# Squares of queries and keys: from ScalarE to GpSimd, for the fifth sequence and later ones

## The chip, the cores and the metric

One Trainium2 chip, one of its cores. The metric is the device time of one execution in microseconds, as the median of several runs. A core has five engines with instruction queues of their own that meet at semaphores: TensorE (PE in the profile; PEld is its weight load), VectorE (DVE), ScalarE (ACT), GpSimd (POOL) and SyncE (SP), which here issues transfers.

## The reference

The input `x` holds 16 sequences of 256 tokens with 128 features. Three layers run one after the other, each on the layer norm of its input: half of a mixture of 8 experts (128 to 512 to 128, one expert for each token), an attention with 16 heads of width 8, and half of the mixture of experts once more. The change lies in the attention's treatment of queries and keys:

```python
q = (x @ wq.T).reshape(B, T, H, hd); k = ...; v = ...
def rms(t):
    var = jnp.mean(t * t, axis=-1, keepdims=True) + EPS
    return g_rms * (t * jax.lax.rsqrt(var))
q, k = (rms(q), rms(k))
q, k = (rope(q), rope(k))
scores = einsum(q, k) * scale + 1.0
y = softmax(scores) @ v
```

`t * t` are the squares of which this document speaks: 128 tokens on the partitions, 256 values (queries and keys of 16 heads) in the free dimension, twice for a sequence (`tt` 0 and 1). The rope turns each half of a head by an angle and commutes with the factor of `rms`, so the kernel turns the raw values and scales them later.

## The kernel before

The program is written out by hand: each engine runs its own list, and the place of a call in a function `step(n)` sets the order. Three stages follow one another: the first mixture of experts (39 tiles of 128 tokens), the attention, and the second mixture.

In the attention each engine runs `step(n)` for n from -20 to 68; step n of TensorE computes the scores of group n, which is a quarter (4 heads) of sequence n // 4. So four steps make one sequence, and a step is known by n mod 4. The same step also works ahead for later groups. For sequence b:

- Normalised input: `xn(b)` on VectorE at step 4b - 20, two instructions that read `X` and `Rstd` from SBUF.
- TensorE projects queries, keys and values of the first 128 tokens at step 4b - 16 and of the other 128 at 4b - 14 (`project_qkv`, L920).
- ScalarE empties the result: `qkv_square` (L1251) writes the squares `Sq`, and `qkv_copy` writes `QkRaw` and `Vg`. The first half is handled at the end of step 4b - 16, the second half's squares at the end of step 4b - 14 and its copies inside step 4b - 13.
- GpSimd's `rope(b, tt)` reads `QkRaw`: a product with `RopeA` (L675), two half-width products with `RopeB` (L680), for `tt` 1 a small one (L687), and the sum of the two (L691). It stands at steps 4b - 16 and 4b - 14; at the latter `split` of sequence b - 1 (L703, L710) comes ahead of it.
- VectorE's `sums(b)` (L1705) adds the squares of each head, at step 4b - 13, and frees ScalarE's `inverse_root(b)` at step 4b - 11. `normalise(b)` (L1715, writes `Rn`) follows at 4b - 10, and GpSimd's `split(b)` waits for it.

The other work of a step n, as the steps of the prediction name it:

- TensorE: scores (L977), scores without a maximum for group n + 6 in two pairs (L954), values of group n - 1 (L1001), and transposes of queries and keys of group n + 7 (L936). The transposes wait for VectorE's first maximum of that step, and the scores of the next step for ScalarE's copy of the transposes.
- ScalarE: two exponentials (L1218), copy of the transposed queries and keys (`QkT`, L1122), small copies.
- VectorE: two maxima (L1732) of 128x1024 from PSUM, and one or two other things. In a step with n mod 4 = 0: `xn`, then `residual` (L1753, L1754), which takes the attention's output for the sequence that is ready. In a step with n mod 4 = 2: `normalise`, at n = 6, 14, 22 and 30 behind four `bn_stats` of reloaded tiles.
- GpSimd: gathers of later tiles (`fetch`, L638, each with a pause L600), and from n = 43 on stores of finished tiles (`place`, L620). The layer norm terms of the second lot of finished tiles (L655 to L665, n = 45) and its router logits (L718 to L723, n = 48) stand there too; VectorE's `one_hot` of step 49 (L1416) waits for the latter.

Of the kernel before, what the change touches and what calls it, by code (L numbers as in the profile page):

```python
# [5 lines left out]
P = 128  # L6
SEQ_TILES = 2
# [77 lines left out]
DRAIN_FIRST = {1: (65,)}  # L85
DRAIN_SECOND = {2: (66, 67), 3: (68,)}
LAST = {"norm": 3, "inverse": 6, "logits": 4, "rank": 9}
XN_AT = {-20: 0, -16: 1, -10: 2, -8: 3, -2: 4}
GATHER_STEP = [0, 1, 2, 3, 4, 5, 6, 9, 10, 13, 14, 17, 18, 21, 22, 25]

def program(nc, x, wqkvT, wpT, g_rms, wrT, br, w1T, b1, w2T, b2,
            ident, before, ones, expert_rank, tile_start, rope_cos, rope_sin, out):
    F32, F32R, I32, BF16 = mybir.dt.float32, mybir.dt.float32r, mybir.dt.int32, mybir.dt.bfloat16
    ALU, ACT, AX = mybir.AluOpType, mybir.ActivationFunctionType, mybir.AxisListType.X
# [11 lines left out]
    with ctx:  # L106
        def sb(name, shape, dt=F32):
            return ctx.enter_context(nc.sbuf_tensor(name, shape, dt))
# [4 lines left out]
        def sem(name):  # L113
            return ctx.enter_context(nc.semaphore(name))
# [100 lines left out]
        QkRaw = sb("QkRaw", [P, 2, SEQ_TILES, 2 * P + N_EXP])  # L215
        Vg = sb("Vg", [P, R_V, SEQ_TILES, N_GRP, GH * 32 + HD + 1])
        Sq = sb("Sq", [P, 2, 2, SEQ_TILES, P])
# [96 lines left out]
        emptied7 = sem("emptied7")  # L314
        qkT_ps = sem("qkT_ps")
        qkT_ready = sem("qkT_ready")
        ss_ready = sem("ss_ready")
        ln_ready = sem("ln_ready")
        rr_ready = sem("rr_ready")
# [29 lines left out]
        def lot(j):  # L349

            return 1 if j < 2 else 2 + j // CH if j >= CH else 2
# [6 lines left out]
        def group(m):  # L358
            return 0 <= m < N_ALL

        def seq(n, lead):

            b, r = divmod(n + lead, N_GRP)
            return b if r == 0 and 0 <= b < N_SEQ else -1
# [39 lines left out]
        def bank_of(*key):  # L404
            return where[key][0]

        def filled(*key):
            return FILLED[where[key][0]], where[key][1]

        def emptied(*key):  # L410
            return EMPTIED[where[key][0]], where[key][1]
# [28 lines left out]
        def tile_expert(k, t):  # L440

            return (Exp2I if k and t >= FULL else ExpI)[0:1, t:t + 1]
# [117 lines left out]
        def _(pool):  # L560
# [106 lines left out]
            def rope(b, tt):  # L667
                u = b % 2
                pool.wait_ge(*emptied(f"qkv{tt}", b))
                if b >= 2:  # L670
                    pool.wait_ge(rn_ready, b - 1)
                if b >= 1:
                    pool.wait_ge(rot_ready, SEQ_TILES * (b - 1) + tt + 1)
                heads = QkRaw[:, u, tt, 0:2 * P].rearrange("p (q h d) -> p q h d", q=2, d=HD)
                nc.gpsimd.tensor_tensor(Rot[:, u, :, tt, :].rearrange("p q (h d) -> p q h d", d=HD), heads,  # L675
                                        RopeA[:, tt].unsqueeze(2).to_broadcast([P, 2, N_HEAD, HD]), ALU.mult)
                half = HD // 2
                swapped = RotB[:, :, tt, :].rearrange("p q (h d) -> p q h d", d=HD)
                for a, c in ((0, half), (half, 0)):
                    last = nc.gpsimd.tensor_tensor(swapped[:, :, :, a:a + half], heads[:, :, :, c:c + half],  # L680
                                                   RopeB[:, tt, :, a:a + half].unsqueeze(2).to_broadcast([P, 2, N_HEAD, half]),
                                                   ALU.mult)
                last.then_inc(rot_terms, 1)
                if tt == 1:
                    j = SEQ_TILES * b
                    pool.wait_ge(std_ready, lot(j))
                    nc.gpsimd.tensor_tensor(Lg[:, j:j + SEQ_TILES, :], QkRaw[:, u, :, 2 * P:2 * P + N_EXP],  # L687
                                            Std[:, j:j + SEQ_TILES].unsqueeze(2).to_broadcast([P, SEQ_TILES, N_EXP]),
                                            ALU.mult).then_inc(logit_in, 1)
                pool.wait_ge(rot_terms, 2 * b + tt + 1)  # L690
                nc.gpsimd.tensor_tensor(Rot[:, u, :, tt, :], Rot[:, u, :, tt, :], RotB[:, :, tt, :], ALU.add).then_inc(rot_ready, 1)  # L691
# [78 lines left out]
            for t in range(S_TILES):  # L770
                if t == LAST["norm"]:
                    lot_layernorm(N_LOT + 1 + LAST_LOT)
                if t == LAST["logits"]:
                    lot_logits(LAST_LOT)
# [7 lines left out]
        def _(pe):  # L782
# [56 lines left out]
            def experts(k):  # L839
# [42 lines left out]
                for t in range(S_TILES + 1):  # L882
# [7 lines left out]
                    if t >= 1:  # L890
                        e = pe.value_load(tile_expert(k, t - 1), min_val=0, max_val=N_EXP - 1)
                    if k and t == LAST["rank"]:
                        rank(LAST_LOT)
# [226 lines left out]
        def _(act):  # L1120
            def copy(dst, src):
                return nc.scalar.activation(dst, src, ACT.Copy)  # L1122
# [23 lines left out]
            def experts(k):  # L1146
# [33 lines left out]
                def run():  # L1180
                    x_evacuate(0)
                    for t in range(S_TILES):
# [6 lines left out]
                        relu(t)  # L1189
                        if k and t == LAST["inverse"]:  # L1190
                            inverse_deviation(N_LOT + len(ROUTE_LOTS))
# [54 lines left out]
            def qkv_square(b, tt):  # L1246
                act.wait_ge(*filled(f"qkv{tt}", b))
                if b >= 2:
                    act.wait_ge(ss_ready, b - 1)
                qk = PS[:, bank_of(f"qkv{tt}", b), 0:2 * P].rearrange("p (q d) -> p q d", q=2)  # L1250
                nc.scalar.activation(Sq[:, b % 2, :, tt, :], qk, ACT.Square)  # L1251

            def qkv_copy(b, tt):
                if b >= 2:
                    act.wait_ge(rot_ready, 2 * (b - 2) + 2)
                if b >= R_V:
                    act.wait_ge(*filled("yu", 2 * (b - R_V) + 1))
                copy(QkRaw[:, b % 2, tt, :], PS[:, bank_of(f"qkv{tt}", b), 0:2 * P + N_EXP])
                copy(Vg[:, b % R_V, tt, :, 0:GH * 32].rearrange("p k (h r) -> p k h r", r=32)[:, :, :, 0:HD],
                     PS[:, bank_of(f"qkv{tt}", b), 2 * P + N_EXP:3 * P + N_EXP].rearrange("p (k h d) -> p k h d", k=N_GRP, d=HD)).then_inc(emptied(f"qkv{tt}", b)[0], 1)  # L1260
# [15 lines left out]

            def first_copy(n):
                if seq(n, 16) >= 0:
                    qkv_square(seq(n, 16), 0)
                    qkv_copy(seq(n, 16), 0)  # L1280

            def second_square(n):
                if seq(n, 14) >= 0:
                    qkv_square(seq(n, 14), 1)

            def second_copy(n):
# [76 lines left out]
        def _(dve):  # L1363
# [335 lines left out]

            def sums(b):  # L1700
                u = b % 2
                dve.wait_ge(*emptied("qkv1", b))
                if b >= 2:
                    dve.wait_ge(rr_ready, b - 1)
                nc.vector.tensor_reduce(Ss[:, u], Sq[:, u].rearrange("p q t (h d) -> p (q t h) d", d=HD),  # L1705
                                        AX, ALU.add).then_inc(ss_ready, 1)
# [61 lines left out]
            def step(n):  # L1768
                if n in RANK_AT:
                    lot_take(RANK_AT[n])  # L1770
                if group(n + MAX_LEAD) and n >= 0:
                    maxima(n + MAX_LEAD, 0)
                if not late(n):
                    small_take(n)
                if late(n) and seq(n - 1, -8) >= 0:
                    residual_stats(seq(n - 1, -8))
                if group(n + MAX_LEAD):
                    maxima(n + MAX_LEAD, 1)
                if n < 0:
                    if n in XN_AT:  # L1780
                        xn(XN_AT[n])
                elif seq(n, 20) >= 0:
                    xn(seq(n, 20))
                if late(n):
                    small_take(n)
                if n in STATS_AT:
                    reload(STATS_AT[n])
                    if STATS_AT[n] < POOL_LOTS:
                        layernorm(STATS_AT[n])
                if seq(n, 13) >= 0:  # L1790
                    sums(seq(n, 13))
                if n in PLACE_AT:
                    lot_place(PLACE_AT[n])
                if n in NORM_AT:
                    layernorm(N_LOT + 1 + NORM_AT[n])
                if n in LOGITS_AT:
                    lot_logits(LOGITS_AT[n])
                if n in HOT_AT:
                    if HOT_AT[n] < len(POOL_LOGITS_AT):
                        dve.wait_ge(lg_ready, HOT_AT[n] + 1)  # L1800
                    one_hot(slice(*ROUTE_LOTS[HOT_AT[n]]))
                if n in PICK_AT:
                    pick(slice(*ROUTE_LOTS[PICK_AT[n]]))
                if n in SEEN_AT:
                    lot_seen(SEEN_AT[n])
                if norm_seq(n) >= 0:
                    normalise(norm_seq(n))
                if n == TABLE_AT:
                    full_table()
# [167 lines left out]
```

## Time and profile before

| | |
|---|---|
| median of 3 runs | 493.08 us (492.8 to 496.94) |
| profiled execution | 493.35 us |
| its span, first to last instruction | 491.5 us |
| PE busy | 433.9 us, 88% |
| DVE busy | 380.5 us, 77% |
| POOL busy | 358.6 us, 73% |
| ACT busy | 349.3 us, 71% |
| chain that ended last, by engine | PE 39%, DVE 19%, POOL 18%, issue 13%, ACT 7% |

Busy time is a sum over the whole program and says little on one stage. The chain follows the last instruction back to what released it, at each step. The attention's steps 0 to 64 lie between 149 and 396 us of the span.

### The profile page before, as it was taken

What the parts mean: (1) busy time and instruction counts of PE and PEld (TensorE: products, weight loads), DVE (VectorE), ACT (ScalarE), POOL (GpSimd) and SP (SyncE); (2) the same over time, 40 slices, a digit from 0 to 9 for tenths busy, and PEclk for the clock granted to TensorE, in tenths of its full rate; (3) what the DMA queues carried; (4) which work ended last, traced back from release to release, by engine and by line L of the source; (5) the groups of instructions that cost most, each with busy time, mean ns of one, the idle gap of its engine ahead of it and who ended that gap; (6) DMA issues with size and microseconds to landing.
All of it is one profiled execution on the core that took longest, in us unless ns stands there. A gap on an engine that the chain in (4) does not pass through costs nothing.

```text
span 491.5 us, 14012 instructions
## 1 busy us (share of the span) xinstructions
PE 433.9 (88%) x4108; PEld 322.8 (66%) x4108; DVE 380.5 (77%) x1037; ACT 349.3 (71%) x782; POOL 358.6 (73%) x579
## 2 busy tenths in 40 slices
PE   7998999969888989999999998988797979799994
PEld 4348998758665555656566655665464459789994
DVE  4785788758787788898988889888788647777772
ACT  4316776757745789999999898888666856557671
POOL 8028898999968588878684874399747616889985
PEclk9798999989997899999999999999899889999998
DMA  7962335251100000000000000000001123223210
GB/s 196 275 255 51 92 89 150 61 164 37 35 24 16 8 25 15 13 8 8 14 14 2 3 3 3 2 13 17 22 25 35 35 57 79 67 84 90 69 37 6
DMA packets 28649, 27.02 MB, mean 55 GB/s; under 512 B 5684, under 2 KB 25947, under 8 KB 28018
## 3 DMA queue, kind: packets, MB, share of 16 engines
q1 hardware_dynamic: 24034, 17.65, 12.1%
q0 software_dynamic: 4544, 8.49, 6.3%
q8 instruction: 36, 0.59, 0.5%
q14 instruction: 35, 0.29, 0.2%
HBM read 16.56 MB, written 12.71 MB: 60 GB/s over the span
## 4 chain that ended last, share of the span: by engine, by line
PE 39%; DVE 19%; POOL 18%; issue 13%; ACT 7%; DMA 1%; DVEq 1%; SPq 1%; ACTq 1%; POOLq 1%
DVE Smax L1732 8%; PE PS L1001 7%; PE PS L860 7%; PE PS L876 6%; PE PS L954 5%; POOL out L629 5%; PE PS L977 4%; POOL Unread L600 4%; PE PS L936 3%; DVE St L1375 2%; ACT Pt L1218 2%; PE PS L920 2%; POOL Pt L607 2%; POOL XX L638 1%; ACT QkT L1122 1%
## 5 line engine op out<-in xcount | busy, mean ns | idle before, releaser
L1732 DVE TENSOR_REDUCE Smax<-PS 128x4 f32<-128x1024 f32 x128 | 155.7, 1223 | 36.3 <-PE PS L954 35.5
L1218 ACT ACTIVATE Pt<-PS 128x1024 f32<-128x1024 f32 x128 | 126.4, 1024 | 20.2 <-PE PS L977 16.9
L876 PE MATMUL PS<-W,HsT 128*128 x624 | 87.4, 284 | 5.7 <-ACT HsT L1163 2.0
L860 PE MATMUL PS<-XsT,Ws 128*128 128x128 f32 x624 | 85.6, 282 | 2.4 <-ACT XsT L1122 2.0
L876 PEld LDWEIGHTS PS<-W,HsT 128*128 128x128 f32 x624 | 77.7, 196 | 10.5 <-issue 9.1
L860 PEld LDWEIGHTS PS<-XsT,Ws 128*128 128x128 f32 x624 | 79.0, 197 | 5.3 <-ACT XsT L1122 2.6
L1001 PE MATMUL PS<-Pt,Vg 128*32 128x256 f32 x1024 | 72.8, 404 | 0.2
L703 POOL TENSOR_TENSOR HL<-Rn,Zero 128x512 fp32r<-128x512 f32 x28 | 35.3, 1282 | 41.8 <-DVE Rn L1715 40.3
L954 PE MATMUL PS<-QkT 24*128 24x256 f32 x512 | 61.3, 312 | 3.0 <-DVE Smax L1732 2.0
L600 POOL MEMSET Unread<- 128x352 f32 (+1 forms) x140 | 62.0, 443 | 0.1
L607 POOL DMA_INDIRECT Pt<-rows,TokI x39 | 40.6, 1040 | 28.6 <-DVE TokI L1573 20.4
L1616 DVE TENSOR_SCALAR HsT<-PS,Bs 128x128 f32<-128x128 f32 x144 | 43.7, 345 | 22.6 <-PE PS L860 21.6
L954 PEld LDWEIGHTS PS<-QkT 24*128 24x128 f32 x512 | 41.3, 190 | 30.1 <-ACT Pt L1218 24.4
L1122 ACT ACTIVATE Ws<-W 128x512 f32 x78 | 49.0, 631 | 10.6 <-DVE ExpI L1580 6.7
L1122 ACT ACTIVATE XsT<-PS 128x128 f32<-128x128 f32 x78 | 21.7, 278 | 46.8 <-PE PS L849 46.6
L1163 ACT ACTIVATE HsT<-PS,Bs 128x128 f32<-128x128 f32 x168 | 51.4, 366 | 4.6 <-PE PS L860 4.5
L629 POOL DMA_INDIRECT out<-AtCol x39 | 38.6, 989 | 21.7 <-DVE AtCol L1627 15.1
L1122 ACT ACTIVATE QkT<-PS 128x512 fp32r<-128x512 f32 x64 | 38.4, 600 | 19.6 <-PE PS L936 18.8
L977 PE MATMUL PS<-QkT 25*128 25x256 f32 x512 | 34.8, 337 | 18.7 <-DVE Smax L1732 9.5
L936 PE MATMUL PS<-I,HL 128*128 128x128 f32 x256 | 43.3, 293 | 6.7 <-DVE Smax L1732 4.5
L977 PEld LDWEIGHTS PS<-QkT 25*128 25x128 f32 x512 | 22.4, 191 | 34.3 <-issue 32.1
L620 POOL DMA_INDIRECT slots<-XX,SlotI x32 | 31.7, 991 | 17.4 <-ACT Pt L1218 12.7
(251 smaller groups left out, 726.4 us busy)
## 6 DMA issues: line engine op xcount, KB each, us to landing
AtCol<-slots SPq DMA_DIRECT2D x39, 65.5 KB, 1.8
rows<-XX SPq DMA_DIRECT2D x8, 288.0 KB, 4.3
XX<-x SPq DMA_DIRECT2D x8, 256.0 KB, 5.1
W<-w1T SPq DMA_DIRECT2D x2, 1024.0 KB, 6.1
W<-w2T SPq DMA_DIRECT2D x2, 1024.0 KB, 9.3
mid<-mid_second SPq DMA_DIRECT2D x1, 1472.0 KB
mid<-Ys SPq DMA_DIRECT2D x16, 64.0 KB
QkT<-NmaxT SPq DMA_DIRECT2D x64, 4.0 KB
```

The source lines that it names most:

```text
L600: nc.gpsimd.memset(Unread[:, 0:columns], 0.0).then_inc(paused, 1)
L629: pool.indirect_dma_start(out, bass.IndirectOffsetOnAxis(ap=Xs2[:, t % R_X2, P + 2:P + 3].bitcast(I32), axis=0), Xs2[:, t % R_X2, 0:P], No ...
L860: last = nc.tensor.matmul(PS[:, h_bank(n) + c // 2, (c % 2) * P:(c % 2 + 1) * P], Ws[:, n % R_WS, c * P:(c + 1) * P], XsT[:, n % 2, :], st ...
L876: last = nc.tensor.matmul(PS[:, y_bank(n), 0:P], HsT[:, n % 2, c, :], W2[:, ds(e * D_FF + c * P, P)], start=(c == 0), stop=(c == FC - 1))
L936: last = nc.tensor.transpose(PS[:, qkT_bank(m), qk * T + tt * P:qk * T + (tt + 1) * P], v, I[:])
L954: last = nc.tensor.matmul(PS[:, max_bank(m, pair) + h % 2, tt * T:(tt + 1) * T], QkT[rows, m % R_QK, 0, tt * P:(tt + 1) * P], QkT[rows, m ...
L977: last = nc.tensor.matmul(PS[:, score_bank(m, h // 2) + h % 2, c * T:(c + 1) * T], QkT[rows, m % R_QK, 1, c * P:(c + 1) * P], QkT[rows, m ...
L1001: last = nc.tensor.matmul(PS[32 * h:32 * h + 32, 6, 0:T], weights[:, c, at:at + 32], Pt[:, m % 2, h, c, :], start=(m % 2 == 0 and c == 0), ...
L1122: return nc.scalar.activation(dst, src, ACT.Copy)
L1163: last = nc.scalar.activation(HsT[:, n % 2, c, :], PS[:, h_bank(n) + c // 2, (c % 2) * P:(c % 2 + 1) * P], ACT.Relu, bias=Bs[:, n % 2, c:c ...
L1218: nc.scalar.activation(Pt[:, m % 2, 2 * pair:2 * pair + 2, :, :].rearrange("p h c t -> p (h c t)"), PS[:, score_bank(m, pair):score_bank(m ...
L1732: nc.vector.tensor_reduce(Smax[:, b % 2, :, at:at + 33:32].rearrange("p t h -> p h t"), PS[:, max_bank(m, pair):max_bank(m, pair) + 2, :]. ...
```

## The change

For sequences from the fifth on (`b >= 4`), ScalarE no longer squares; GpSimd squares `QkRaw` inside `rope`, between the products and the sum. VectorE's `sums(b)` waits for the two squares on GpSimd and stands at step 4b - 12 in place of 4b - 13, behind `xn` and `residual` of that step. `qkv_copy` takes over the wait for the projection that `qkv_square` had.

```diff
+ACT_SQUARES = 4
 def rope(b, tt):                                       # GpSimd
     ...
                 last.then_inc(rot_terms, 1)
+                if b >= ACT_SQUARES:
+                    pool.wait_ge(ss_ready, b - 1)
+                    qk = QkRaw[:, u, tt, 0:2 * P].rearrange("p (q d) -> p q d", q=2)
+                    nc.gpsimd.tensor_tensor(Sq[:, u, :, tt, :], qk, qk, ALU.mult).then_inc(sq_ready, 1)
                 if tt == 1:
 def qkv_copy(b, tt):                                   # ScalarE
+    if b >= ACT_SQUARES:
+        act.wait_ge(*filled(f"qkv{tt}", b))
 def first_copy(n):
     if seq(n, 16) >= 0:
-        qkv_square(seq(n, 16), 0)
+        if seq(n, 16) < ACT_SQUARES:
+            qkv_square(seq(n, 16), 0)
         qkv_copy(seq(n, 16), 0)
 def second_square(n):
-    if seq(n, 14) >= 0:
+    if 0 <= seq(n, 14) < ACT_SQUARES:
 def sums(b):                                           # VectorE
-    dve.wait_ge(*emptied("qkv1", b))
+    if b < ACT_SQUARES:
+        dve.wait_ge(*emptied("qkv1", b))
+    else:
+        dve.wait_ge(sq_ready, SEQ_TILES * (b - ACT_SQUARES + 1))
 # in VectorE's step(n), behind xn and residual:
-    if seq(n, 13) >= 0:
+    if 0 <= seq(n, 13) < ACT_SQUARES:
         sums(seq(n, 13))
+    if seq(n, 12) >= ACT_SQUARES:
+        sums(seq(n, 12))
```

VectorE, one sequence from `normalise` (step n mod 4 = 2) to the first maximum of the step n mod 4 = 1, before:

```order
L1715 TENSOR_TENSOR Rn<-Rot,Rr 128x512 [waits hl_ready,rot_ready,rr_ready]
L1732 TENSOR_REDUCE Smax<-PS 128x2x2 [waits filled6,smax_ps] x2
L1705 TENSOR_REDUCE Ss<-Sq 128x64 [waits rr_ready,emptied7]
L1732 TENSOR_REDUCE Smax<-PS 128x2x2 [waits filled6,smax_ps] x2
L1695 SCALAR_TENSOR_TENSOR XN<-XX,Mean 128x128 [waits filled7,ln_rstd]
L1695 SCALAR_TENSOR_TENSOR XN<-XX,Mean 128x128
L1753 TENSOR_TENSOR XX<-PS,XX 128x2x128 [waits logit_in,filled6]
L1754 TENSOR_TENSOR Lg<-PS,Lg 128x16
L1732 TENSOR_REDUCE Smax<-PS 128x2x2 [waits filled6,smax_ps]
```

and now (line numbers are those of the changed kernel):

```order
L1727 TENSOR_TENSOR Rn<-Rot,Rr 128x512 [waits hl_ready,rot_ready,rr_ready]
L1744 TENSOR_REDUCE Smax<-PS 128x2x2 [waits filled6,smax_ps] x4
L1704 SCALAR_TENSOR_TENSOR XN<-XX,Mean 128x128 [waits filled7,ln_rstd]
L1704 SCALAR_TENSOR_TENSOR XN<-XX,Mean 128x128
L1765 TENSOR_TENSOR XX<-PS,XX 128x2x128 [waits logit_in,filled6]
L1766 TENSOR_TENSOR Lg<-PS,Lg 128x16
L1717 TENSOR_REDUCE Ss<-Sq 128x64 [waits rr_ready,sq_ready]
L1744 TENSOR_REDUCE Smax<-PS 128x2x2 [waits filled6,smax_ps]
```

The sum of squares left the place between two pairs of maxima and stands between the residual and the next step's first maximum.

GpSimd, the rope part of the second 128 tokens and the gather behind it, before:

```order
L675 TENSOR_TENSOR Rot<-QkRaw,RopeA 128x2x128 [waits rot_ready,rn_ready,emptied7]
L680 TENSOR_TENSOR RotB<-QkRaw,RopeB 128x2x16x4 x2
L687 TENSOR_TENSOR Lg<-QkRaw,Std 128x16 [waits std_ready]
L691 TENSOR_TENSOR Rot<-Rot,RotB 128x2x128 [waits rot_terms]
L638 DMA XX<-mid,SlotI 128x128
```

and now:

```order
L677 TENSOR_TENSOR Rot<-QkRaw,RopeA 128x2x128 [waits rot_ready,rn_ready,emptied7]
L682 TENSOR_TENSOR RotB<-QkRaw,RopeB 128x2x16x4 x2
L689 TENSOR_TENSOR Sq<-QkRaw 128x2x128 [waits ss_ready]
L693 TENSOR_TENSOR Lg<-QkRaw,Std 128x16 [waits std_ready]
L697 TENSOR_TENSOR Rot<-Rot,RotB 128x2x128 [waits rot_terms]
L640 DMA XX<-mid,SlotI 128x128
```

One product is added, and everything behind it on GpSimd comes later by it.

## Rows read from the trace of the kernel before

**Rows 1.** Busy time by stretch: PE, PEld, DVE, ACT, POOL, then granted clock, DMA.

```profile
240.60:255.80 15.20, 13.80 (x163) 8.78 (x161) 13.55 (x20) 13.86 (x28) 12.94 (x26) 1.00 0.05 13
```

**Rows 2.** Timeline of PE, steps 24 to 26: start, us, engine, line, [idle before].

```profile
247.21 0.63 PE L1031 MATMUL PS<-Wp,YnT 128*128 128x136 f32 x4
247.77 0.51 PE L977 MATMUL PS<-QkT 25*128 25x256 f32 x8
...
249.99 0.66 PE L936 MATMUL PS<-I,HL 128*128 128x128 f32 x4
...
251.54 0.51 PE L977 MATMUL PS<-QkT 25*128 25x256 f32 x8 [0.45 <-DVE Smax L1732]
```

**Rows 3.** Timeline of ACT, the same steps.

```profile
247.41 0.38 ACT L1251 ACTIVATE Sq<-PS 128x256 f32<-128x256 f32 x1
...
248.33 1.94 ACT L1218 ACTIVATE Pt<-PS 128x1024 f32<-128x1024 f32 x2
250.69 0.60 ACT L1122 ACTIVATE QkT<-PS 128x512 fp32r<-128x512 f32 x1 [0.41 <-PE PS L936]
```

**Rows 4.** Timeline of DVE, steps 23 to 25.

```profile
243.41 0.67 DVE L1705 TENSOR_REDUCE Ss<-Sq 128x64 f32<-128x512 f32 x1
244.74 1.23 DVE L1732 TENSOR_REDUCE Smax<-PS 128x4 f32<-128x1024 f32 x1 [0.65 <-PE PS L954]
246.17 1.23 DVE L1732 TENSOR_REDUCE Smax<-PS 128x4 f32<-128x1024 f32 x1 [0.21 <-PE PS L954]
247.31 0.77 DVE L1695 SCALAR_TENSOR_TENSOR XN<-XX,Mean 128x128 f32<-128x128 f32 x2
...
248.34 0.16 DVE L1754 TENSOR_TENSOR Lg<-PS,Lg 128x16 f32<-128x16 f32 x1
248.55 1.23 DVE L1732 TENSOR_REDUCE Smax<-PS 128x4 f32<-128x1024 f32 x1
```

**Rows 5.** Timelines of POOL, DVE and PE, steps 20 and 21.

```profile
231.01 0.72 POOL L691 TENSOR_TENSOR Rot<-Rot,RotB 128x256 f32<-128x256 f32 x1
...
233.20 0.16 DVE L1754 TENSOR_TENSOR Lg<-PS,Lg 128x16 f32<-128x16 f32 x1
233.53 1.23 DVE L1732 TENSOR_REDUCE Smax<-PS 128x4 f32<-128x1024 f32 x1 [0.17 <-PE PS L954]
...
234.90 0.63 PE L936 MATMUL PS<-I,HL 128*128 128x128 f32 x4
```

**Rows 6.** Timeline of POOL, rope of the second 128 tokens beside rows 4.

```profile
245.30 0.74 POOL L675 TENSOR_TENSOR Rot<-QkRaw,RopeA 128x256 f32<-128x256 f32 x1
245.99 0.78 POOL L680 TENSOR_TENSOR RotB<-QkRaw,RopeB 128x128 f32<-128x128 f32 x2
...
246.89 0.74 POOL L691 TENSOR_TENSOR Rot<-Rot,RotB 128x256 f32<-128x256 f32 x1
```

**Rows 7.** Timelines of DVE and POOL in the ramp, short windows.

```profile
144.04 0.41 DVE L1695 SCALAR_TENSOR_TENSOR XN<-XX,Mean 128x128 f32<-128x128 f32 x1
144.38 0.88 DVE L1695 SCALAR_TENSOR_TENSOR XN<-XX,Mean 128x128 f32<-128x128 f32 x1
144.38 0.72 POOL L691 TENSOR_TENSOR Rot<-Rot,RotB 128x256 f32<-128x256 f32 x1
```

**Rows 8.** Chain that ended last, POOL's first and last pieces, then DVE: start, us.

```profile
318.88 2.52 POOL HL L703 x2
...
344.61 0.29 POOL Lg L723
344.92 0.23 DVE Mx L1416
```

**Rows 9.** Timeline of DVE, where that piece hands over.

```profile
344.92 0.22 DVE L1416 TENSOR_REDUCE Mx<-Lg 128x8 f32<-128x64 f32 x1 [0.68 <-POOL Lg L723]
```

**Rows 10.** Timelines of DVE, step 38, and PE, step 41.

```profile
298.35 2.35 DVE L1732 TENSOR_REDUCE Smax<-PS 128x4 f32<-128x1024 f32 x2
...
310.09 0.18 PE L824 MATMUL PS<-SeenE,Ahead 128*128 128x8 bf16 x1 [0.21 <-DVE Lg L1754]
```

**Rows 11.** Busy time by stretch, behind that hand-over, columns as in rows 1.

```profile
352.00:358.00 6.00, 5.54 (x41) 3.45 (x40) 2.57 (x3) 3.19 (x5) 5.43 (x8) 0.50 0.07 22
```

More of the change, by code:

```diff
@@ L316, in program @@
         qkT_ready = sem("qkT_ready")
+        sq_ready = sem("sq_ready")
         ss_ready = sem("ss_ready")
```

## The prediction

> **What bounds the kernel now.** I read the chain that ended last first: between 149 and 318 us it changes from engine to engine several times in a step, so no engine is the bound by itself. The busy times by stretch say the same [rows 1]: of 15.2 us for four steps TensorE is busy for 13.80, ScalarE 13.86, VectorE 13.55, GpSimd 12.94. So the question is which wait ends last at the places that the change touches, and for that I read the timelines engine by engine, for a sequence's four steps (24 to 27, and 20 to 23, the two kinds that alternate).
>
> A step of TensorE begins with the scores L977. Step 25's start at 247.77 and follow L1031, which ends at 247.84 and overlaps by 0.07: here TensorE runs through and waits for nobody [rows 2]. Step 26's start at 251.54. That row names VectorE, but ScalarE's copy QkT ends at 251.29 [rows 3], 0.25 before it; that copy itself sat idle for 0.41 until TensorE's transposes L936, which run from 249.99 on. The transposes need VectorE's first maximum of the step, which runs from 248.55 to 249.78 [rows 4], so only 0.21 us before they start. The loop to watch is therefore: VectorE's first maximum of the step with n mod 4 = 1, transposes, copy, next scores. Whatever delays that maximum by more than 0.21 delays all engines.
>
> Late in the attention there is another bound. From 318.88 to 344.90 the chain is GpSimd alone [rows 8], and VectorE waits 0.68 for it at the end [rows 9].
>
> **What ScalarE saves.** 24 squares of 0.38 us [rows 3], 9.1 us of busy time. In the first step of a sequence the square stands at 247.41, and two copies and the next exponentials at 248.33 follow it. These need the scores that started at 247.77 and took 0.51, until 248.28 [rows 2]; without the square ScalarE would wait for them, and 0.05 is gained at most. In the third step the square stands behind the copy QkT for which TensorE waits. So I take nothing for it; the bounds are 0 and the 9.1.
>
> **What GpSimd gains in work.** The trace shows no square on GpSimd. The nearest row is the product of the same size, L675: it starts at 245.30 and the next instruction at 245.99, so 0.69 each [rows 6]. The half-width product takes 0.39 (0.78 for two), a lower bound; the double-width L703 takes 1.26 [rows 8], an upper one. I take 0.69. While GpSimd has idle time in each sequence the 24 x 0.69 = 16.6 us are covered, and two things are left.
>
> First, the **late chain**. Three squares lie in it: the second half of sequence 14 (step 42) and both halves of sequence 15 (steps 44 and 46). 3 x 0.69 = 2.1 us, with 1.2 and 3.8 as bounds. All of it arrives, since VectorE already waits there. The sums of steps 44 and 48 run in that wait: sums of step 48 has to wait for sequence 15's second square, but what it loses is less than the 2.1 by which GpSimd is late anyway. If this cover were gone they would cost some 0.5 each. [...]
>
> Second, **XN beside GpSimd**. In the ramp one XN that starts together with L691 takes 0.88 and ends at 145.26, 0.16 after L691's end at 145.10; the XN just before it took 0.41 [rows 7]. So an XN does not get through while such an instruction runs. In step 24 the pair of XN starts at 247.31 and ends at 248.08 [rows 4], while L691 runs until 247.63 [rows 6]. With the square L691 starts 0.69 later and ends at 248.32; the second XN would end at 248.48, 0.40 later than now. The Trainium skill (SBUF — State Buffer, section on the two separate sides) states this as a rule: a VectorE instruction with two SBUF inputs and a GpSimd instruction that reads SBUF exclude each other for a whole instruction. By that rule the trace agrees, 0.88 against 0.41, and it speaks against this change; without it the sum below would be 2.0 us smaller (five steps of 0.40).
>
> **What VectorE's move costs.** Sums leaves a place where it costs nothing: it runs for 0.67 from 243.41, and behind it VectorE is idle for 0.65 until TensorE's scores arrive [rows 4]. It goes to the place ahead of the first maximum of the loop above. An instruction on VectorE starts 0.09 before the end of the one ahead (247.31 against 246.17 + 1.23), so sums adds 0.58, and starts 0.07 after Lg.
>
> - Steps 8, 16, 24 and 32 (four tiles are reloaded two steps ahead of each, and the rope runs late, into XN): the maximum moves from 248.55 to 248.34 + 0.40 + 0.07 + 0.58 = 249.39, 0.84 later. Less the 0.21 of slack, 0.63 arrive. Four times: 2.5 us.
> - Steps 12, 20 and 28: L691 ends at 231.73 [rows 5], with the square at 232.42, about where XN begins, so XN is left alone. The maximum moves from 233.53 to 233.20 + 0.07 + 0.58 = 233.85. The slack is 234.90 - 234.76 = 0.14, and 0.18 arrive. Three times: 0.5 us.
> - Step 36: behind it VectorE works without a pause through step 37's one-hot and step 38's two maxima [rows 10], so there is no slack; 0.65 less the 0.21 that lay between Lg and the maximum is 0.44, and some of XN's delay: 0.5 us.
> - Step 40: TensorE's rank L824 waits for Lg [rows 10], so XN's 0.40 pass to TensorE directly, and sums hides behind them: 0.4 us.
> - Step 4 has no residual yet, and VectorE has room: 0.
>
> Are squares late for sums? In step 24 the square would end at 246.68 + 0.73 = 247.41; sums wants it at 248.81. Even 1.26 would do. Behind sums on VectorE stand the maxima, so a late square would be dear, but only step 48 has one.
>
> **Sum.** 2.5 + 0.5 + 0.5 + 0.4 = 3.9 for VectorE's place and XN, 2.1 for the late chain: 6.0 us. The profiled execution took 493.35 us, 0.27 above the median of 493.08; its span is 491.5, and what lies around it does not change. So 499.35 for such an execution, and 499.1 for the median.
>
> **Rivals.** A measurement of this kernel can tell about 1%, 4.9 us, from no change: below 488.2 is faster, above 498.0 slower.
>
> 1. ScalarE sets the pace after all, and the change is faster. For it: ScalarE is the busiest engine in the stretch, and each step's scores follow its copy by 0.25. Against: its idle 0.41 ahead of that copy, and exponentials that wait for scores. If all 24 squares came off the path, 9.1 less: 484.0; if only the 12 of the first step, 4.6 less: 488.5. It decides if exponentials start earlier when the square is gone. Chance 0.08, most of it below 488.2.
> 2. VectorE's delay stays in the slack. If XN is not held (GpSimd waits in its place) and sums fits into idle time that the rows show as waits for TensorE, only the late chain is left: 493.1 + 2.1 = 495.2; with half of VectorE's cost 497. For it: VectorE is idle for over 1.5 us in four steps. Against: the idle time lies in other steps. Chance 0.27.
> 3. The clock. Behind the late chain TensorE's granted clock is 0.50 (1.2 GHz) from 352 to 358, with 5.54 us of work [rows 11], after TensorE had waited for VectorE. A longer wait for GpSimd could make a second such stretch; it would cost up to half of 5.5, 2.8 us more: 502. Chance 0.15.
> 4. The squares are late for sums in every sequence, because GpSimd's square is far dearer than any row shows. VectorE would stand still for what exceeds 1.4 us in eight or more sequences: 505 and more. Chance 0.04.
>
> That the change does less than it says I leave out: the order of the instructions shows all 24 squares moved.
>
> **Numbers.** The forecast has 0.46, and within it 497.5 to 501. Of that some 0.05 lies under 498.0. Faster: 0.07. Within 1%: 0.27 + 0.05 + 0.01, so 0.33. Slower: 0.60. The range 494.6 to 502.6 takes in rival 2 with the lower bound of the late chain (493.1 + 1.2, rounded up) and rival 3; left out are rivals 1 and 4 and the edges, 0.2 together.
>
> **What the changed profile would show.** Right: the first maximum of steps 9, 17 and 25 starts right behind sums, without a wait for TensorE; the second XN of steps 8, 16 and 24 ends 0.16 after a GpSimd instruction and the pair takes over 1.1 us; four steps take 15.7 and 15.3 us in turn instead of 15.1; ScalarE waits longer for scores in front of its exponentials; the GpSimd part of the chain before the one-hot of step 49 is 2.1 longer. Wrong: XN pairs as short as now; transposes that start no later after their scores than now; exponentials that start earlier after the scores; sums that wait for GpSimd before step 48.

## The result and the profile after

The changed kernel took 500.12 us as the median of 4 executions (497.21 to 503.82), the kernel before 492.94 us on the same chip (492.69 to 496.94): a ratio of 1.018 with a 95% interval of [1.0121, 1.0239]. The interval lies above 1, so the change is slower; whether by more than 2% it leaves open. Six more executions on another chip gave a median of 501.8 us (one of them took 1310.87) and 1.0219 [1.0136, 1.0301]. The ratios, here and below, take in only executions within 1.5% of the fastest of the same kernel, the medians all of them. The forecast was 499.1 us.

The profiled execution of the changed kernel took 497.21 us, only 3.86 above that of before. It had more of the full clock: a mean granted clock of 0.963 against 0.951. Over 109 executions of all kernels in this study (three far ones left out: 1310.87 and 1323.81 us at a clock of 1.00, 502.91 at 0.834), a line of time against mean granted clock, with one slope for all and a level for each kernel, falls by 0.32 us for 0.001 of clock; 0.012 are 3.9 us, and 3.86 + 3.9 is 7.7. At an equal clock of 0.955 that line gives, as an estimate, 492.9 us before and 499.2 after, 6.3 +- 0.7 more. So a single pair of executions would have shown half of the cost, and below I read lengths of steps rather than ends.

First the work. The page of the changed kernel, section 1 (busy us, share of the span, instructions):

```profile
PE 432.2 (87%) x4108; PEld 320.5 (65%) x4108; DVE 381.7 (77%) x1037; ACT 343.1 (69%) x758; POOL 372.7 (75%) x603
```

GpSimd's 358.6 have become 372.7, ScalarE's 349.3 have become 343.1. ScalarE's busiest groups in both kernels (busy us, mean ns of one, then idle us just before them and what ended it), before:

```profile
L1218 ACT ACTIVATE Pt<-PS 128x1024 f32<-128x1024 f32 x128 | 126.4, 1024 | 20.2 <-PE PS L977 16.9 <-DVE Ys L1627 1.9
L1122 ACT ACTIVATE QkT<-PS 128x512 fp32r<-128x512 f32 x64 | 38.4, 600 | 19.6 <-PE PS L936 18.8
```

and after:

```profile
L1224 ACT ACTIVATE Pt<-PS 128x1024 f32<-128x1024 f32 x128 | 126.5, 1024 | 23.7 <-PE PS L983 20.7 <-DVE Ys L1636 1.9
L1128 ACT ACTIVATE QkT<-PS 128x512 fp32r<-128x512 f32 x64 | 38.4, 599 | 26.0 <-PE PS L942 25.1
```

24 squares of 0.38 (9.1) were taken away, and ScalarE's busy time, in which overlapping instructions count once, fell by 6.2. In front of these two instructions it waits 3.5 and 6.4 us longer for TensorE. Not all of that is the relief: the kernel in which the squares are only left out (below) waits 4.3 longer in front of the exponentials and no longer in front of QkT. So the 6.4 belong to the longer steps, in which the transposes that QkT copies come later.

Now the place of [rows 4], VectorE from the last maxima of step 24 to the first of step 25, in the changed kernel (start, us, engine, line, [idle before]):

```profile
247.61 1.23 DVE L1744 TENSOR_REDUCE Smax<-PS 128x4 f32<-128x1024 f32 x1 [0.21 <-PE PS L960]
248.75 1.09 DVE L1704 SCALAR_TENSOR_TENSOR XN<-XX,Mean 128x128 f32<-128x128 f32 x2
249.76 0.41 DVE L1765 TENSOR_TENSOR XX<-PS,XX 128x256 f32<-128x256 f32 x1
250.09 0.16 DVE L1766 TENSOR_TENSOR Lg<-PS,Lg 128x16 f32<-128x16 f32 x1
250.18 0.67 DVE L1717 TENSOR_REDUCE Ss<-Sq 128x64 f32<-128x512 f32 x1
250.77 1.21 DVE L1744 TENSOR_REDUCE Smax<-PS 128x4 f32<-128x1024 f32 x1
```

GpSimd beside it:

```profile
248.15 0.62 POOL L689 TENSOR_TENSOR Sq<-QkRaw 128x256 f32<-128x256 f32 x1
248.90 0.78 POOL L697 TENSOR_TENSOR Rot<-Rot,RotB 128x256 f32<-128x256 f32 x1
```

and TensorE, which answers to [rows 2]:

```profile
249.21 0.51 PE L983 MATMUL PS<-QkT 25*128 25x256 f32 x8
...
250.31 1.07 PE L1007 MATMUL PS<-Pt,Vg 128*32 128x256 f32 x16 [0.37 <-DVE Lg L1766]
...
252.12 0.63 PE L942 MATMUL PS<-I,HL 128*128 128x128 f32 x4 [0.32 <-DVE Smax L1744]
253.64 0.51 PE L983 MATMUL PS<-QkT 25*128 25x256 f32 x8 [0.45 <-DVE Smax L1744]
```

The pair of XN takes 1.09 instead of 0.77 and ends at 249.84, which is 0.16 after GpSimd's sum (248.90 + 0.78 = 249.68): the same 0.16 as in the ramp [rows 7]. Sums stands behind Lg, the maximum behind sums without a pause, and the transposes now wait 0.32 for it. From step 25's scores to its transposes it is 2.91 us (252.12 - 249.21), before 2.22 [rows 2]. Step 25 takes 4.43 us instead of 3.77.

There is a second way to TensorE, which the prediction does not have for these steps. The values (L1007) write to the PSUM bank that the residual reads and wait for Lg, the residual's last instruction. They start 0.06 after its end at 250.25. They did so before, too, 0.06 after Lg's end at 248.50, so there was no slack on this way; their weight load before:

```profile
248.56 0.59 PEld L1001 LDWEIGHTS PS<-Pt,Vg 128*32 128x32 f32 x16 [0.26 <-DVE Lg L1754]
```

The values started 0.79 after the scores (248.56 - 247.77) and now start 1.10 after them (250.31 - 249.21), 0.31 later, as much as XN was held. The transposes stand behind the values on TensorE; here the maximum comes later still and decides.

In step 20, the other kind, XN is left alone and only sums delays the maximum. VectorE:

```profile
233.40 0.60 DVE L1704 SCALAR_TENSOR_TENSOR XN<-XX,Mean 128x128 f32<-128x128 f32 x2
...
234.39 0.68 DVE L1717 TENSOR_REDUCE Ss<-Sq 128x64 f32<-128x512 f32 x1
234.98 1.22 DVE L1744 TENSOR_REDUCE Smax<-PS 128x4 f32<-128x1024 f32 x1
```

and TensorE:

```profile
236.34 0.63 PE L942 MATMUL PS<-I,HL 128*128 128x128 f32 x4 [0.31 <-DVE Smax L1744]
```

The maximum ends at 236.20, the transposes start 0.14 later. Those 0.14 stood in the rows of before as well (234.90 - 234.76, [rows 5]).

How much longer each step is than before, from one start of scores to the next:

| kernel | steps 9, 17, 25, 33 | 13, 21, 29 | 37 | 41 | 45 | all of steps 4 to 37 |
|---|---|---|---|---|---|---|
| changed | 0.66 to 0.72 | 0.34 | 0.33 | 1.08 | 0.34 | 4.13 |
| only sums moved | 0.33 to 0.39 | 0.34 to 0.35 | 0.36 | 0 | 0.34 | 2.80 |
| only squares added | 0.30 to 0.36 | 0 | 0 | 0.38 | 0 | 1.26 |
| squares left out | 0 | 0 | 0 | 0 | 0 | 0.04 |
| XN earlier | 0.23 to 0.34 | 0.34 to 0.35 | 0.23 | 0 | 0.35 | 2.33 |
| sums first | 0 | 0 | 0 | 0 | 0 | 0.45 |
| late squares on ScalarE | 0.66 to 0.71 | 0.34 | 0.33 | 0.45 | 0 | 4.11 |
| sums first, late on ScalarE | 0 | 0 | 0 | 0 | 0 | 0.09 |

A 0 stands for less than 0.12. The rows below the first are those of the experiments. Steps in a stretch of half clock are left out of the columns (step 40 of "only sums moved", step 44 of the last). Of the 0.45 of "sums first", 0.36 lie in step 4, ahead of which the pair of XN took 1.63 in that execution.

Step 41 is the surprise. VectorE in step 40, after:

```profile
312.48 1.70 DVE L1704 SCALAR_TENSOR_TENSOR XN<-XX,Mean 128x128 f32<-128x128 f32 x2
```

GpSimd there, after:

```profile
312.56 0.74 POOL L697 TENSOR_TENSOR Rot<-Rot,RotB 128x256 f32<-128x256 f32 x1
313.25 0.78 POOL L677 TENSOR_TENSOR Rot<-QkRaw,RopeA 128x256 f32<-128x256 f32 x1
```

and GpSimd at the same place before:

```profile
308.49 0.72 POOL L691 TENSOR_TENSOR Rot<-Rot,RotB 128x256 f32<-128x256 f32 x1
309.94 0.73 POOL L675 TENSOR_TENSOR Rot<-QkRaw,RopeA 128x256 f32<-128x256 f32 x1 [0.73 <-ACT Vg L1122]
```

Before, GpSimd's next rope part waited 0.73 for ScalarE's copies. Now the sum ends later, and without the square ahead of them the copies are early: counted from step 41's scores the product starts at 0.32 (313.25 - 312.93) instead of 0.56 (309.94 - 309.38). It follows the sum at once (no gather lies between any more), and XN is held by two instructions in a row: its pair ends at 314.18, 0.15 after the second one's end at 314.03. So the relief of ScalarE bought a loss there.

The late chain, which answers to [rows 8] and [rows 9]. GpSimd, after:

```profile
323.52 2.52 POOL L709 TENSOR_TENSOR HL<-Rn,Zero 128x512 fp32r<-128x512 f32 x2 [7.46 <-DVE Rn L1727]
...
337.33 0.75 POOL L663 TENSOR_SCALAR Var<-Var 128x8 f32<-128x8 f32 x1
```

the same instruction before:

```profile
331.65 0.21 POOL L661 TENSOR_SCALAR Var<-Var 128x8 f32<-128x8 f32 x1
```

and VectorE, after:

```profile
337.33 0.68 DVE L1727 TENSOR_TENSOR Rn<-Rot,Rr 128x512 f32<-128x512 f32 x1
...
346.67 0.69 DVE L1717 TENSOR_REDUCE Ss<-Sq 128x64 f32<-128x512 f32 x1 [1.26 <-POOL Sq L689]
...
351.70 0.22 DVE L1425 TENSOR_REDUCE Mx<-Lg 128x8 f32<-128x64 f32 x1 [0.97 <-POOL Lg L729]
```

From the start of HL on GpSimd to VectorE's Mx it is 28.18 us (351.70 - 323.52), before 26.04 [rows 8]. In step 48 sums waits 1.26 for its square, the only such wait of all 12.

Behind the hand-over TensorE's clock fell again. Busy time by stretch, after (columns as in [rows 1]):

```profile
355.00:356.00 1.00, 0.61 (x12) 0.57 (x12) 0.93 (x10) 0.46 (x3) 0.00 (x0) 1.00 0.20 67
356.00:359.00 3.00, 3.00 (x25) 1.45 (x23) 2.28 (x6) 1.88 (x2) 1.99 (x2) 0.51 0.02 5
359.00:360.00 1.00, 0.89 (x6) 0.65 (x4) 0.98 (x1) 0.29 (x1) 0.92 (x2) 0.77 0.00 0
```

Some 3.5 us at the lower level (1.2 GHz) where before had over 6 [rows 11]; step 52 is 2.12 shorter for it. This is a part of what the profiled execution gave back.

### The profile page after: what moved, and what is told of

The parts are those of the page before. It is cut to its first block, busy times and chain, and to the rows that moved or that the text cites. A ratio compares the mean times of both kernels' runs of the same rounds, so it can differ in the third digit from the quotient of the medians.

```text
span 495.4 us, 13990 instructions
## 1 busy us (share of the span) xinstructions
PE 432.2 (87%) x4108; PEld 320.5 (65%) x4108; DVE 381.7 (77%) x1037; ACT 343.1 (69%) x758; POOL 372.7 (75%) x603
## 4 chain that ended last, share of the span: by engine, by line
PE 41%; DVE 22%; issue 14%; POOL 14%; ACT 6%; DVEq 1%; POOLq 0%; ACTq 0%
DVE Smax L1744 11%; PE PS L1007 8%; PE PS L866 7%; PE PS L882 7%; PE PS L960 5%; POOL out L631 5%; PE PS L983 4%; POOL Unread L602 4%; PE PS L942 3%; ACT Pt L1224 2%; DVE St L1384 2%; POOL Pt L609 2%; ACT QkT L1128 2%; PE PS L919 1%; POOL XX L640 1%
## 5 line engine op out<-in xcount | busy, mean ns | idle before, releaser
L882 PEld LDWEIGHTS PS<-W,HsT 128*128 128x128 f32 x624 | 76.7, 193 | 11.3 <-issue 10.2
L866 PEld LDWEIGHTS PS<-XsT,Ws 128*128 128x128 f32 x624 | 78.0, 195 | 5.5 <-ACT XsT L1128 2.9
L1007 PE MATMUL PS<-Pt,Vg 128*32 128x256 f32 x1024 | 72.8, 404 | 1.5 <-DVE Lg L1766 1.4
```

The source lines that it names most:

```text
L866: last = nc.tensor.matmul(PS[:, h_bank(n) + c // 2, (c % 2) * P:(c % 2 + 1) * P], Ws[:, n % R_WS, c * P:(c + 1) * P], XsT[:, n % 2, :], st ...
L882: last = nc.tensor.matmul(PS[:, y_bank(n), 0:P], HsT[:, n % 2, c, :], W2[:, ds(e * D_FF + c * P, P)], start=(c == 0), stop=(c == FC - 1))
L1007: last = nc.tensor.matmul(PS[32 * h:32 * h + 32, 6, 0:T], weights[:, c, at:at + 32], Pt[:, m % 2, h, c, :], start=(m % 2 == 0 and c == 0), ...
```

## The experiments

The first four were timed beside each other (before: 493.75 us, median of 13), the other four on another chip (492.69, median of 29). "At 0.955" is the difference to before by the line of time against granted clock described above.

**Sums one step later, nothing else.**

```diff
 # before.py, VectorE's step(n)
-                if seq(n, 13) >= 0:
+                if 0 <= seq(n, 13) < LATE_SUMS:          # 4
                     sums(seq(n, 13))
+                if seq(n, 12) >= LATE_SUMS:
+                    sums(seq(n, 12))
```

> The kernel before with one part of the change: sums of sequences 4 to 15 stands one step later, behind xn and residual; ScalarE still squares, GpSimd has no square. If the place of sums on VectorE carries the cost: TensorE's step pairs with a sums ahead of them grow by 0.3 to 0.4 each from step 9 to step 37, 3 us in all, nothing at step 41 and nothing in the late chain; 496. If the squares on GpSimd carry it: no step grows, 493. If the half-clock stretches carry it: no step grows in the attention, and the time follows the granted clock alone.

496.65 us, 1.0119 [1.0021, 1.0216]; at 0.955 +3.1 +- 1.0. VectorE at the place of [rows 4]:

```profile
248.85 0.77 DVE L1696 SCALAR_TENSOR_TENSOR XN<-XX,Mean 128x128 f32<-128x128 f32 x2
...
249.96 0.67 DVE L1706 TENSOR_REDUCE Ss<-Sq 128x64 f32<-128x512 f32 x1
250.55 1.21 DVE L1733 TENSOR_REDUCE Smax<-PS 128x4 f32<-128x1024 f32 x1
```

XN keeps its 0.77, and each sequence pays 0.33 to 0.39. The move costs by itself, without a square on GpSimd.

**Squares on GpSimd added, nothing else.** ScalarE keeps its squares, and GpSimd writes the same product into a tile that nobody reads.

```diff
 # before.py, rope(b, tt)
                 last.then_inc(rot_terms, 1)
+                if b >= EXTRA:                           # 4
+                    ...
+                    nc.gpsimd.tensor_tensor(Spare[:], qk, qk, ALU.mult).then_inc(sq_ready, 1)
```

> The kernel before with the other part alone: GpSimd squares at the same place into a spare tile that nobody reads; ScalarE still squares, sums stands where it stood. If XN held by GpSimd and the late chain carry the rest: the XN pair of steps 8, 16, 24 and 32 takes 1.1 instead of 0.77 and the maximum behind it comes 0.3 later, of which 0.2 arrive each time; up to 1 us at step 40; the hand-over to step 49's one-hot comes 2 us later; 3.5 us in all, 496.5. If only the place of sums counts: 493.

498.71 us, 1.02 [1.0106, 1.0295]; at 0.955 +3.1 +- 0.9. VectorE at the same place, sums being where it was before:

```profile
242.63 1.08 DVE L1705 SCALAR_TENSOR_TENSOR XN<-XX,Mean 128x128 f32<-128x128 f32 x2
...
244.05 1.21 DVE L1742 TENSOR_REDUCE Smax<-PS 128x4 f32<-128x1024 f32 x1
```

and GpSimd:

```profile
242.76 0.81 POOL L701 TENSOR_TENSOR Rot<-Rot,RotB 128x256 f32<-128x256 f32 x1
```

XN's pair grows to 1.08, ends (243.71) 0.14 after GpSimd's sum (243.57), and steps 9, 17, 25 and 33 get 0.30 to 0.36 longer; the steps in which the sum misses XN do not. This delay does not reach TensorE by the maximum, as was expected. TensorE:

```profile
243.09 0.51 PE L987 MATMUL PS<-QkT 25*128 25x256 f32 x8
...
244.18 1.07 PE L1011 MATMUL PS<-Pt,Vg 128*32 128x256 f32 x16 [0.36 <-DVE Lg L1764]
...
245.62 0.66 PE L946 MATMUL PS<-I,HL 128*128 128x128 f32 x4
```

The maximum ends at 245.26, 0.36 before the transposes start, so they do not wait for it. They stand behind the values, which wait for Lg: from the scores to the values it is 1.09 us instead of 0.79, to the transposes 2.53 instead of 2.22.

HL to Mx takes 28.19 us (315.24 to 343.43). The two halves add up: 2.80 + 1.26 = 4.06 in steps 4 to 37, against 4.13 of the change. At step 41 they do not (0.38 against 1.08).

**ScalarE's squares left out** (sequences 4 to 15).

```diff
 # before.py
-                    qkv_square(seq(n, 16), 0)
+                    if seq(n, 16) < KEPT:                # 4
+                        qkv_square(seq(n, 16), 0)
 def second_square(n):
-                if seq(n, 14) >= 0:
+                if 0 <= seq(n, 14) < KEPT:
 def qkv_copy(b, tt):                                   # takes over the square's wait
+                if b >= KEPT:
+                    act.wait_ge(*filled(f"qkv{tt}", b))
```

> The kernel before without the squares on ScalarE for sequences 4 to 15 (left out altogether: sums adds stale values), all else as it was. If ScalarE does not set the pace: 493, within 0.5, and the exponentials wait longer for the scores. If it does: up to 9 us less, 484 to 488.

493.3 us over 10 executions, 1.0006 [0.9936, 1.0075]; at 0.955 -0.1 +- 0.6. ScalarE there:

```profile
244.91 1.94 ACT L1219 ACTIVATE Pt<-PS 128x1024 f32<-128x1024 f32 x2 [0.35 <-PE PS L978]
247.24 0.60 ACT L1123 ACTIVATE QkT<-PS 128x512 fp32r<-128x512 f32 x1 [0.39 <-PE PS L937]
```

The exponentials, which before followed the copies without a pause [rows 3], now wait 0.35 for the scores, and no step is shorter by more than 0.06. Over the whole program the two groups shown for the changed kernel read here:

```profile
L1219 ACT ACTIVATE Pt<-PS 128x1024 f32<-128x1024 f32 x128 | 126.4, 1024 | 24.5 <-PE PS L978 21.6 <-DVE Ys L1631 1.9
L1123 ACT ACTIVATE QkT<-PS 128x512 fp32r<-128x512 f32 x64 | 38.4, 600 | 19.4 <-PE PS L937 18.6
```

Taking 9 us of work off the busiest engine of the stretch is worth nothing that shows.

**XN one step earlier**, in the change, where sums used to stand.

```diff
 # after.py, VectorE's step(n)
-                elif seq(n, 20) >= 0:
+                elif 0 <= seq(n, 20) < EARLY_XN:         # 6
                     xn(seq(n, 20))
+                elif seq(n, 21) >= EARLY_XN:
+                    xn(seq(n, 21))
```

> The changed kernel with xn of sequences 6 to 15 one step earlier, in the place that sums left. If VectorE's path ahead of the first maximum carries the loss: steps 9 to 37 are as long as in the kernel before, the late chain and step 45 still cost 2.5 us; 495.5. If the squares on GpSimd delay VectorE or the transposes in another way: the steps stay as long as in the changed kernel, 500.

499.71 us, 1.0115 [0.9991, 1.024]; at 0.955 +3.7 +- 0.9. VectorE in steps 23 to 25:

```profile
246.76 1.38 DVE L1705 SCALAR_TENSOR_TENSOR XN<-XX,Mean 128x128 f32<-128x128 f32 x2
...
251.22 0.42 DVE L1766 TENSOR_TENSOR XX<-PS,XX 128x256 f32<-128x256 f32 x1 [0.48 <-PE PS L1038]
...
252.24 1.21 DVE L1745 TENSOR_REDUCE Smax<-PS 128x4 f32<-128x1024 f32 x1
```

XN is still held by GpSimd, even longer than in the change (its pair takes 1.38), but now in step 23, which is no longer than before; step 41's loss is gone with it. I had not seen what comes next: the residual waits 0.48 for TensorE's projection, and sums still stands behind it, ahead of the maximum. Of the 4.13 in steps 4 to 37, 2.33 stayed, against what I expected, and that pointed to the next kernel.

**Sums first**: XN as in the last one, and sums in the place that XN left, ahead of the residual, where VectorE waits in any case.

```diff
 # the kernel of the last experiment, VectorE's step(n), behind xn
+                if seq(n, 12) >= ACT_SQUARES:
+                    sums(seq(n, 12))
                 ...                                      # residual
-                if seq(n, 12) >= ACT_SQUARES:
-                    sums(seq(n, 12))
```

> The changed kernel with xn one step earlier and sums in xn's old place, ahead of the residual. The run with xn earlier alone kept 0.23 and 0.34 a sequence, with the residual waiting 0.48 for TensorE's projection and sums behind it. If it is the instructions between the residual and the first maximum that cost: steps 9 to 37 as long as in the kernel before, within 0.05, with sums done while VectorE would wait for the projection; step 41 up to 0.4 longer; the late chain still 2 us; 495.5 at a granted clock of 0.955. If sums delays VectorE wherever it stands in that step: the 0.34 stay, 499.

490.21 us over 12 executions, 1.0003 [0.9962, 1.0045]; at 0.955 +1.3 +- 0.6. VectorE around step 24's residual, and at step 48:

```profile
243.28 0.69 DVE L1718 TENSOR_REDUCE Ss<-Sq 128x64 f32<-128x512 f32 x1
...
244.42 1.23 DVE L1745 TENSOR_REDUCE Smax<-PS 128x4 f32<-128x1024 f32 x1
...
337.78 0.69 DVE L1718 TENSOR_REDUCE Ss<-Sq 128x64 f32<-128x512 f32 x1 [1.92 <-POOL Sq L690]
...
343.11 0.21 DVE L1426 TENSOR_REDUCE Mx<-Lg 128x8 f32<-128x64 f32 x1
```

The maximum again starts 0.78 after step 25's scores (243.64), as it did before (248.55 - 247.77), and every step from 9 to 45 has its old length within 0.1. The squares stand on GpSimd as in the change, and XN's pair is still held (1.38 in step 23); it was the place of VectorE's instructions that cost. The late loss remains: HL to Mx 28.21 us (314.90 to 343.11). But here Mx follows VectorE's own work without a wait, 0.32 after GpSimd's Lg ended at 342.79: at step 48 sums waits 1.92 for its square and now holds the residual behind it.

**Squares of sequences 14 and 15 back on ScalarE**, their sums back in the old place.

```diff
 # after.py: rope, qkv_copy, sums and VectorE's step(n)
-                if b >= ACT_SQUARES:
+                if ACT_SQUARES <= b < POOL_END:          # 14
 # first_copy and second_square
-                    if seq(n, 16) < ACT_SQUARES:
+                    if not ACT_SQUARES <= seq(n, 16) < POOL_END:
```

> The changed kernel with the squares of the last two sequences (14 and 15) back on ScalarE, and their sums back in the old place. If the late chain is made of GpSimd's squares: the hand-over to step 49's one-hot comes 4 us after the kernel before's, counted from step 4, in place of 7.4; step 45 no longer 0.34 longer, sums of step 48 no longer waits; 497 at a clock of 0.955. If the late loss is something else, such as the clock's stretches: 499 to 500, with the late steps as in the changed kernel.

496.71 us over 12 executions, 1.0028 [0.9971, 1.0085]; at 0.955 +5.2 +- 0.6. The ratio and the line disagree, since the six executions in the ratio had more of the full clock (0.965 to 0.979) than the other six (0.945 to 0.953); I go by the steps. HL to Mx is 26.08 us (319.51 to 345.59), steps 45 and 49 have their old length, steps 9 to 37 are as long as in the change. VectorE and GpSimd in step 40:

```profile
309.08 1.08 DVE L1705 SCALAR_TENSOR_TENSOR XN<-XX,Mean 128x128 f32<-128x128 f32 x2
```

```profile
309.20 0.81 POOL L698 TENSOR_TENSOR Rot<-Rot,RotB 128x256 f32<-128x256 f32 x1
310.10 0.73 POOL L678 TENSOR_TENSOR Rot<-QkRaw,RopeA 128x256 f32<-128x256 f32 x1
```

With sequence 14's square on ScalarE again the next product starts 0.09 after the sum's end (310.01) and no longer right behind it; XN's pair ends at 310.16, held by the sum alone (1.08, not 1.70), and step 41 loses 0.45 instead of 1.08.

**Both**: sums first, and the late squares on ScalarE.

> The two before together. If VectorE's place, XN held by GpSimd and the late chain are all that the change costs, and ScalarE's relief is worth nothing: every step from 4 to 53 as in the kernel before, but for up to 0.4 at step 41; the same time as before, 493 to 494 at a clock of 0.955. If ScalarE's relief is worth something once the rest is undone: under 492.

491.35 us over 12 executions, 0.9972 [0.9912, 1.0032]; at 0.955 0.0 +- 0.6 (one execution at a clock of 0.834 left out). All that the change cost is taken back, and nothing that shows is gained over the kernel before: 20 of the 24 squares are off ScalarE here too. In the profiled execution a stretch of half clock falls into step 44 (1.56 longer), GpSimd then waits 0.67 for ScalarE's copies, and HL to Mx is 26.83 us.

**The change once more**, unedited, beside the last three.

> The changed kernel as it is. If its loss is in the steps and not in the clock's stretches: at the same granted clock as a run of the kernel before, 5 to 7 us more, and steps 9 to 46 longer by the same 0.66 and 0.34 as in its first profile. If its loss came by the stretches: no difference at the same clock.

501.8 us, 1.0219 [1.0136, 1.0301]. The steps of the first three columns of the table repeat to 0.02: 0.66, 0.68, 0.66, 0.71 and four times 0.33 or 0.34; HL to Mx is 28.03 us. Step 41 can't be compared: a stretch of half clock from 313.2 to 320.1 falls into it and step 42 (1.36 and 2.27 longer). The lengths of steps are a property of the order, the end also of where the clock falls.

## Why the prediction was right, and where it was not

The forecast direction and the two mechanisms behind it, XN held by GpSimd and sums ahead of the maximum, are shown by the runs; several sizes were off, and that the sum came out so near is in part luck.

**ScalarE's saving, taken as 0.** Shown: with the squares left out 34 steps together change by 0.04 us. Rival 1 is out.

**The square on GpSimd, 0.69.** It takes 0.60 to 0.62; the next instruction starts 0.57 to 0.58 later. I took the product of the same size in the rows; this one has the same operand twice and is cheaper, and no run here shows why. The Trainium skill (GPSIMD Engine Reference, section 3.1) gives 4497 ns for an addition of two tiles of 2048 columns. Scaled to 256 that is an estimate of 0.56, which is near the square here; the addition of that size, GpSimd's sum L691, takes 0.72 [rows 5] and 0.74 [rows 6].

**XN beside GpSimd, 0.40 in each even sequence.** The mechanism is shown, by the kernel with squares alone and by the rows 0.14 to 0.16 behind GpSimd's end; the size was 0.32 (1.09 - 0.77), less mainly because the square was cheaper by 0.12. How it reaches TensorE I had only in part: not by the maximum alone but also by Lg and the values, which had no slack, as the kernel with squares alone shows. The rule that I set beside it (the Trainium skill, SBUF — State Buffer, the two separate sides) holds in this case in both directions: in the late chain it is GpSimd that is held, L663 running for 0.75 from 337.33 with VectorE's Rn in the same place, where the same instruction took 0.21 before. In the kernel with squares alone it is the instruction before it that meets Rn (0.75), in the repeat of the change the one behind it (0.63). Rival 2, in which XN is not held and the delay stays in the slack, is out.

**Sums ahead of the maximum.** 0.63 forecast for steps 8, 16, 24 and 32, 0.66 to 0.72 measured; 0.18 forecast for steps 12, 20 and 28, 0.34 measured. The step that failed is "the slack is 234.90 - 234.76 = 0.14": that is not slack. The transposes start 0.14 after the maximum's end when they do wait for it, so the 0.14 is the way from VectorE's end to TensorE's start, and the true slack was 0 in the odd sequences and 0.07 in the even ones. The kernel with only sums moved bears it out: its maximum starts 1.24 after step 25's scores (249.31) instead of 0.78, 0.46 later, and 0.33 to 0.39 arrive, where a slack of 0.21 would have left 0.25. In the even ones the cheaper square hid the error. Step 36: 0.5 forecast, 0.33 measured.

**Step 40: 0.4 forecast, 1.08 measured.** The largest error, 0.7. I moved GpSimd's instructions by the added square only and did not ask what the removed one sets free: ScalarE's copies came earlier, so GpSimd's next product did, by 0.24. The rows of before had the wait (0.73 for ScalarE), and I had not read them.

**The late chain: 2.1 forecast, 2.14 measured**, but of other parts. The three squares make 1.61 (0.58, 0.46 and 0.57; the second covers a short wait that was there before), and L663's hold 0.54 more. Two errors of half a microsecond cancel: that this term fits is luck. That the sums of steps 44 and 48 run in its cover held: step 45 is 0.34 longer, and the hand-over shows nothing of it, since 5.28 us of delay at HL (323.52 - 318.88, and the 0.64 by which this execution was ahead at step 4) and 2.14 give the 7.42 that are there at Mx (351.70 - 344.92 + 0.64).

**Sum.** 6.0 forecast; 4.13 + 1.13 (steps 38 to 43, nearly all step 41) + 2.14 = 7.40 measured at Mx, counted from step 4. At the end 7.18 lie between the medians, and 6.3 +- 0.7 at equal clock. That this is so near to 6.0 is in part luck as well: VectorE's place and XN cost 5.26 where 3.9 were forecast. In the profiled execution the 7.42 at Mx are 4.5 at the end (spans of 495.4 and 491.5 us, and the 0.64), and the trace shows stretches of half clock where they went. Step 52 lost one. In steps 58 to 60, which are 1.12 shorter, 0.64 longer and 1.41 longer, one moved from 378.8 to 385.7 (before) to 386.8 to 393.6. Behind the attention before has one from 399.3 to 402.7 and the changed kernel none; from step 63's scores to the end it took 97.7 us instead of 100.1. Why 7.40 at Mx and 6.3 at equal clock differ stays open.

**The clock, rival 3.** The stretch at half clock behind the hand-over was shorter, not longer, in the profiled execution. It went against the rival, but I don't count this as shown for all executions: the mean granted clock of the changed kernel's nine lay between 0.920 and 0.966, of before between 0.938 and 0.976. The medians are 0.945 and 0.955. If the change itself brings the lower clock, that adds to the 6.3: by the line 0.010 are 3.2 us, and on the second chip the two medians of time lie 9.1 apart. Nine executions don't decide it.

## What to carry to other kernels

Where a loop goes round several engines, an instruction costs by its place and not by its length: the same sum of squares costs 0 in front of a wait and 0.34 behind it, XN held for 1.38 costs nothing one step earlier, and work taken off the busiest engine is worth nothing as long as that engine then waits. Before a gap is called slack, look in a step that really waits for how late the waiting engine starts after the end of what it waits for (here 0.14), and take that off. And of an edit that moves work between engines ask both questions: what does the added work hold up, and what will the freed engine now release earlier, and beside whom.

## What was not expected of the hardware

In the changed kernel a product of a tile with itself takes GpSimd 0.61 us on average (24 of them), a product of the same size with a second tile (L677) 0.74. A GpSimd instruction of 128x8 that meets VectorE's Rn takes 0.75 instead of 0.21. And the same program differs by 2.5% from one execution to the next (485.5 to 497.9 us for the kernel before, one of 1323.81 left out) with its mean granted clock between 0.976 and 0.938, more than the change costs.
